# Joined turns between stages, and the tokens' places made on TensorE at the attention's end

## Chip, core and metric

One core of a Trainium2 chip runs the whole program as one launch. The metric is the device time of one execution in microseconds (us). Three executions of the kernel before took 1667.34 (the median), 1662.26 and 1670.05 us.

## What is computed

The input x has 2048 tokens of 512 float32 numbers. Two layers follow each other:

```python
xn = layernorm(x)
x = x + attention(xn) + ffn0(xn)     # layer 0
xn = layernorm(x)
x = x + lightning(xn) + ffn1(xn)     # layer 1

# attention: 16 heads of 32, causal softmax with ALiBi, then @ Wo + bo
# ffn0: each token goes to one of two experts, by a sign:
top_expert = argmax(softmax(xn @ Wg.T))
out0 = gelu(xn @ W0a.T + b0a) @ W0b.T + b0b
out1 = relu(xn @ W1a.T + b1a) @ W1b.T + b1b
y = where(top_expert == 0, out0, out1)
# lightning: chunked linear attention with decay, gate, norm, @ Wo
# ffn1: w1, w2, w3 are rounded to -1, 0, 1 (x1, x2 -> sigmoid(x1) * x2 -> w3)
```

The experts are not both computed for each token. The tokens are sorted by expert into 17 tiles of 128 places (each expert's tokens fill whole tiles, empty places are left at the ends), and `rt.idx`, 128 x 17 whole numbers, says for each place which token lies there, or a dump row past the tokens where none does.

## The kernel before

Six stages run one after the other. Each is a `Stage`, which holds its tiles and semaphores, with one block, in which every engine (PE, DVE, ACT, POOL, SP) has its own program:

- qkv (0 to 168 us): layer norm of x and the three projections. For each of four chunks of 512 tokens it stores xn, q, k (in two parts, high and low) and v to HBM, and loads the first pair of heads' q and k back. At its end SP waits until all stores have landed.
- att (168 to 792 us): the attention, 8 pairs of heads, 40 steps a pair, 320 steps `g` in all. First, `unit` products on PE with their row maxima on DVE (L1030) run ahead by 28 steps (`LEAD`); DVE turns the maxima of a chunk, and SP moves them by small DMAs (L844) into the rows of q, so that the `score` products (L952) come out with the maximum taken off. DVE masks the diagonal (L1039), ACT takes the exponent (L1008), and PE multiplies by v (L966, `sums`). Units and scores share a ring of 7 PSUM banks in an order written out by `ScoreRing`: PE, DVE and ACT all follow it, each product waits until its two banks are free. Pair 0 makes its own units and those of pair 1 within its 40 steps. After the last step's units, some 28 steps before the end, DVE has only masks to do. ACT copies a chunk's sums out (L992), SP stores them. POOL meanwhile loads the second pair's q and k, splits 16 pieces of expert weights into high and low parts (L151, L160) and rounds w1, w2, w3 (`Quantizer`, L202 to L265).
- proj (793 to 870 us): the output projection with the residual, stored as x1a. POOL fetches the first two tiles of xn by `rt.idx`.
- moe (871 to 1098 us): the experts, tile by tile. POOL gathers rows of xn and of x1a and puts the results back by `rt.idx` with indirect DMAs.
- lin (1099 to 1426 us): the linear attention. glu (1427 to 1672 us): ffn1.

A stage ends so: `nc.Block()` closes with a barrier of all engines, ahead of which each engine, POOL too, runs a DRAIN (L55); then POOL clears the stage's semaphores (L57), and a second barrier of all engines follows (L58).

The routing (`Router`) lies in the attention. SP loads its constants (L731, L732) at the start. DVE counts the tokens of expert 0 (L737 to L743) before it takes its first unit, PE makes the ranks with three products (L752 to L754) after the first 12 units, DVE takes them (L760), and after unit 40 DVE makes each token's place in 12 small steps (L768 to L779). POOL fills `token_of_place` in HBM with dump rows (L785), scatters the token numbers to it, 16 indirect DMAs of 128 numbers of 4 bytes (L789), waits for them and loads the table back into `rt.idx` (L792). Only then does it start on the weights. DVE uses `rt.idx` first in proj (L1272).

Of the kernel before, what the change touches and what calls it, by code (L numbers as in the profile page):

```python
# [18 lines left out]
BF16 = mybir.dt.bfloat16  # L19
# [5 lines left out]
P = 128  # L25
T = 2048
# [18 lines left out]
class Stage:  # L45


    def __init__(self, nc, name):
        self.nc, self.name, self.stack, self.sems = nc, name, ExitStack(), []
# [20 lines left out]
    def block(self):  # L70
        return self.stack.enter_context(self.nc.Block())
# [285 lines left out]
class Early:  # L357
# [7 lines left out]

    @staticmethod
    def operands(t):
        return t[0:KROWS, 1, :].rearrange("p (h t) -> p h t", h=2)
# [25 lines left out]
def normed_qkv_stage(nc, early, carried, w_d, bqk_d, bv_d, x_d, cst_d, wg_d, diff, xn_d, qh_d, ql_d, kh_d, kl_d, v_d, alibi):  # L394
# [3 lines left out]
    with Stage(nc, "qkv") as st:  # L398
        wh, wl = st.sb("wh", [P, KT, 2 * D], F32R), st.sb("wl", [P, KT, 2 * D], F32R)
# [13 lines left out]
        vb = st.sb("vb", [P, TT, D])  # L413
# [11 lines left out]
        v_stored = st.sem("v_stored")  # L425
# [5 lines left out]
        def _(sp):  # L431
# [33 lines left out]
            for sem, n in [(xn_stored[i], NCH // 2) for i in range(2)] + [  # L465
                    (qk_stored[i], NCH * 2 * NQK // 4) for i in range(4)] + [
                    (v_stored, NCH), (pair_in, NCH * 2 * LOADS)]:
# [146 lines left out]
LEAD, FIRST_LEAD, PLACES_AT = 28, 12, 40  # L614
# [49 lines left out]
class ScoreRing:  # L664
# [42 lines left out]
class Router:  # L707


    PAD, PARTS = 16, 5  # L710

    def __init__(self, st, rt, room, cst_d, ids_d, dump_d, idx_d, out):
        self.rt, self.cst_d, self.ids_d, self.dump_d, self.idx_d, self.out = rt, cst_d, ids_d, dump_d, idx_d, out
        cst, work = room
        self.cst = cst[:, 0:2 * P + NT + QT]
        self.tri, self.ones = cst[:, 0:P], cst[:, P:2 * P]
        self.starts, self.token = cst[:, 2 * P:2 * P + NT], cst[:, 2 * P + NT:2 * P + NT + QT]
        n = self.PARTS * (self.PAD + QT)
        self.counts_all = work[:, 0:n]
        self.counts = work[:, 0:n].rearrange("p (a b) -> p a b", a=self.PARTS)  # L720
        self.rank, self.place = work[:, n:n + NT], work[:, n + NT:n + NT + QT]
        self.base = work[:, n + 2 * NT:n + 2 * NT + 1]
        self.ids, self.pos = st.sb("ids", [P, QT], U32), st.sb("pos", [P, QT], U32)
        self.cst_in, self.ids_in = st.sem("route_cst_in"), st.sem("route_ids_in")
# [3 lines left out]
        self.filled, self.scattered, self.idx_in = st.sem("route_filled"), st.sem("route_scattered"), st.sem("route_idx_in")  # L728

    def load(self, eng):  # L730
        eng.dma_start(self.cst, self.cst_d).then_inc(self.cst_in, 16)  # L731
        eng.dma_start(self.ids[:], self.ids_d).then_inc(self.ids_in, 16)  # L732
# [14 lines left out]
    def ranks(self, pe):  # L747
# [4 lines left out]
        pe.matmul(self.out[:, 0:QT], self.tri, self.counts[:, 0, pad:], start=True, stop=False)  # L752
        pe.matmul(self.out[:, 0:QT], self.ones, self.counts[:, 4, pad - 1:pad - 1 + QT], start=False, stop=True)
        pe.matmul(self.out[:, QT:NT], self.ones, self.counts[:, 4, pad + QT - 1:pad + QT], start=True, stop=True  # L754
                  ).then_inc(self.ranked, 1)

    def take_ranks(self, dve):

        dve.wait_ge(self.ranked, 1)
        dve.tensor_copy(self.rank, self.out[:, 0:NT]).then_inc(self.rank_taken, 1)  # L760

    def places(self, dve):

        rt, first = self.rt, self.counts[:, 0, self.PAD:]
        dve.wait_ge(self.rank_taken, 1)
        rank = self.rank[:, 0:QT]
        chain = Chain(dve, self.step, 0)
        chain.link(dve.tensor_scalar(rt.f0[:], self.starts, self.rank[:, QT:NT], None, ALU.is_lt))  # L768
# [10 lines left out]
        dve.tensor_copy(self.pos[:], self.place).then_inc(self.placed, 1)  # L779

    def store(self, pool):

        by_place = self.idx_d.rearrange("(j p) a -> p (j a)", p=P)
# [1616 lines left out]
```

## Time and profile before

| | us |
|---|---|
| median of three executions | 1667.34 |
| profiled execution | 1674.07 |
| its span, first to last instruction | 1672.3 |
| mean granted clock of PE | 0.969 of full |
| PE busy | 1547.4 (93%) |
| DVE busy | 985.3 (59%) |
| POOL busy | 658.8 (39%) |
| ACT busy | 591.8 (35%) |

Busy time is the time in which the engine had an instruction under way; PE's ends are modelled. The granted clock has two levels here: 1.00 is 2.4 GHz, 0.50 is 1.2 GHz. In a timeline a row is one instruction, or several alike in a row (x8), with start and duration; the bracket tells how long the engine stood idle before it, and what ended that. SPq, ACTq and POOLq rows are work of the engines' queues (DMA issues, semaphores, DRAINs).

### The profile page before, as it was taken

The page shows a single profiled execution, that of the slowest core. Times are in us where ns is not written, and L with a number is a line of the kernel's source. Part 1 is how long each engine was busy: PE and PEld are TensorE (multiplying, and loading weights), DVE is VectorE, ACT ScalarE, POOL GpSimd, SP SyncE. Part 2 cuts the span into 40 slices and gives each one's busy share as a digit, 9 for nine tenths or more (in the row PEclk, how much of TensorE's full clock was granted, in tenths as well). Part 3 has the DMA queues.
Part 4 walks back from the last instruction along what each step waited for, and adds up shares of the span by engine and source line. Part 5 has one row for each costly group of instructions (what it writes and reads, how often), then busy time and mean ns, then how long its engine had stood idle before and what let it go on. Part 6 is the DMA issues. An engine that isn't in the chain of part 4 may idle for free. (4 is left out here: it accounts for less than half of the span.)

```text
span 1672.3 us, 22094 instructions
## 1 busy us (share of the span) xinstructions
PE 1547.4 (93%) x7890; PEld 1077.2 (64%) x7890; DVE 985.3 (59%) x1706; ACT 591.8 (35%) x1124; POOL 658.8 (39%) x552
## 2 busy tenths in 40 slices
PE   5998969999999999998889999949999998999998
PEld 4887534555555555543667888837777776788887
DVE  7673867878878887770436656535655546232332
ACT  3121224555555555546212222244424232222221
POOL 4100237695885979670318676613110201000000
PEclk9999689999999999999899999979999999999999
DMA  6877513645545464320762122153030222420210
GB/s 235 248 253 210 104 39 97 155 97 121 148 105 102 117 166 101 82 90 11 254 217 69 64 80 66 51 176 122 8 127 0 77 58 81 145 79 22 101 51 25
DMA packets 105053, 182.03 MB, mean 109 GB/s; under 512 B 29433, under 2 KB 45833, under 8 KB 104293
## 3 DMA queue, kind: packets, MB, share of 16 engines
q1 hardware_dynamic: 87176, 119.13, 25.1%
q0 software_dynamic: 14128, 53.88, 11.2%
q10 hardware_dynamic: 3640, 7.61, 1.2%
q8 instruction: 65, 1.06, 0.3%
q14 instruction: 44, 0.35, 0.1%
HBM read 118.56 MB, written 61.75 MB: 108 GB/s over the span
## 5 line engine op out<-in xcount | busy, mean ns | idle before, releaser
L1008 ACT ACTIVATE att_probs<-att_ring 128x512 f32<-128x512 f32 (+3 forms) x640 | 297.0, 538 | 297.9 <-DVE att_ring L1039 172.2
L1030 DVE TENSOR_REDUCE att_maxes<-att_ring 128x2 f32<-128x1024 f32 (+7 forms) x366 | 338.9, 946 | 71.4 <-PE att_ring L931 62.9
L966 PE MATMUL att_outp<-att_probs,att_vs 128*64 128x512 f32 (+3 forms) x1280 | 274.7, 551 | 0.3 <-ACT att_att L992 0.3
L966 PEld LDWEIGHTS att_outp<-att_probs,att_vs 128*64 128x64 f32 x1280 | 78.9, 138 | 122.0 <-issue 69.1
L931 PE MATMUL att_ring<-route_wbh,route_wah 100*128 100x512 f32 (+2 forms) x320 | 103.8, 408 | 12.3 <-PEq L58 6.4
L1731 DVE TENSOR_TENSOR glu_hid<-glu_sig,glu_u 128x512 f32<-128x512 f32 x44 | 30.2, 687 | 141.3 <-PE glu_u L1671 141.3
L931 PE MATMUL att_ring<-moew_wbl,moew_wal 100*128 100x512 f32 (+2 forms) x320 | 98.0, 381 | 15.4 <-ACT att_probs L1008 12.1
L952 PE MATMUL att_ring<-route_wah,route_wbh 102*128 102x512 f32 (+2 forms) x320 | 105.8, 406 | 3.5 <-issue 2.4
L952 PE MATMUL att_ring<-moew_wal,moew_wbl 102*128 102x512 f32 (+2 forms) x320 | 100.9, 399 | 2.6 <-DVE att_maxes L1030 2.5
L2301 POOL TENSOR_TENSOR lin_sig<-lin_o_copy,lin_sig 128x512 f32<-128x512 f32 x16 | 20.4, 1276 | 208.5 <-ACT lin_o_copy L2161 208.5
L1039 DVE TENSOR_TENSOR att_ring<-att_ring,route_cst 128x128 f32<-128x128 f32 x256 | 64.5, 297 | 59.2 <-PE att_ring L952 51.8
L952 PEld LDWEIGHTS att_ring<-route_wah,route_wbh 102*128 102x128 f32 x320 | 55.4, 193 | 67.1 <-issue 44.9
L952 PEld LDWEIGHTS att_ring<-moew_wal,moew_wbl 102*128 102x128 f32 x320 | 53.7, 188 | 63.6 <-issue 32.1
L1744 POOL DMA_DIRECT2D out<-glu_y x3 | 2.4, 798 | 218.0 <-DVE glu_y L1715 218.0
L931 PEld LDWEIGHTS att_ring<-route_wbh,route_wah 100*128 100x128 f32 x320 | 63.5, 206 | 31.8 <-DVE att_maxes L1030 8.7
L931 PEld LDWEIGHTS att_ring<-moew_wbl,moew_wal 100*128 100x128 f32 x320 | 60.1, 191 | 32.2 <-ACT att_probs L1008 17.5
L1542 POOL TENSOR_SCALAR moe_r<-moe_z,route_f 128x512 f32<-128x512 f32 x34 | 69.8, 2057 | 4.1 <-DVE moe_z L1468 2.7
L1670 PE MATMUL glu_u<-tail_xh,tail_up 128*128 128x512 f32 x176 | 68.5, 389 | 2.0 <-DVEq L1723 2.0
L1683 PE MATMUL glu_down<-glu_w,glu_hh 128*128 128x512 f32 x176 | 68.6, 390 | 0.4 <-DVE glu_hl L1733 0.4
L1684 PE MATMUL glu_down<-glu_w,glu_hl 128*128 128x512 f32 x176 | 68.5, 389 | 0.0
L1671 PE MATMUL glu_u<-tail_xl,tail_up 128*128 128x512 f32 x176 | 68.5, 389 | 0.0
L1670 PE MATMUL glu_u<-glu_xh,tail_up 128*128 128x512 f32 x176 | 68.5, 389 | 0.0
(282 smaller groups left out, 3443.4 us busy)
## 6 DMA issues: line engine op xcount, KB each, us to landing
att_q_raw<-in_w POOLq DMA_DIRECT2D x48, 352.0 KB, 3.9
w_ternary<-att_q_out POOLq DMA_DIRECT2D x24, 352.0 KB, 2.6
tail_up<-w_ternary SPq DMA_DIRECT2D x22, 256.0 KB, 4.8
xn<-qkv_x SPq DMA_DIRECT2D x4, 1024.0 KB, 7.3
q_hi<-qkv_hi SPq DMA_DIRECT2D x16, 256.0 KB, 3.8
q_lo<-qkv_lo SPq DMA_DIRECT2D x16, 256.0 KB, 4.7
k_hi<-qkv_hi SPq DMA_DIRECT2D x16, 256.0 KB, 2.9
k_lo<-qkv_lo SPq DMA_DIRECT2D x16, 256.0 KB, 3.7
```

The source lines that it names most:

```text
L931: last = pe.matmul(out[h][:, 0:cover], qs[par][0:SROWS, h, t * P:(t + 1) * P], ks[par][0:SROWS, h, g * CH:g * CH + cover], start=True, sto ...
L952: last = pe.matmul(out[h][:, start:CH], ks[par][:, h, kt * P:(kt + 1) * P], qs[par][:, h, c * CH + start:(c + 1) * CH], start=True, stop=True)
L966: last = pe.matmul(outp[v_cols(h), off:CH], vs[p % 2][:, kt, v_cols(h)], probs[:, g % 4, h, off:CH], start=kt == 0, stop=kt == TT * (c + 1 ...
L1008: act.activation(probs[:, g % 4, h, off:CH], ring[:, rg.banks["score", g][h], off:CH], ACT.Exp).then_inc(exped, 1)
L1030: last = dve.tensor_reduce(maxes[:, hs, t, g:g + 1], banks[:, :, 0:width], AX.X, ALU.max)
L1039: dve.tensor_tensor(block, block, neg_k, ALU.add).then_inc(masked, 1)
L1542: pool.tensor_scalar(r[:, half, :], z[:, half, :], 0.0, rt.f1[:, j:j + 1], ALU.max, ALU.mult).then_inc(relued, 1)
L1670: pe.matmul(u[:, n % 2, :], w[:, f, k, :], xh[c % 2][:, k, :], start=k == 0, stop=False)
L1671: last = pe.matmul(u[:, n % 2, :], w[:, f, k, :], xl[c % 2][:, k, :], start=False, stop=k == KT - 1)
L1683: pe.matmul(down[:, t, :], hh[:, n % 2, s], w3[:, f, :], start=f == 0, stop=False)
L1684: last = pe.matmul(down[:, t, :], hl[:, n % 2, s], w3[:, f, :], start=False, stop=f == GT - 1)
L1731: dve.tensor_tensor(hid[:, n % 2, :], sig[:, n % 2, :], u2[:, n % 2, :], ALU.mult).then_inc(hid_ready, 1)
```

## The change

1. The turns: `Block(no_gpsimd_drain=True)` closes a block with a barrier ahead of which POOL runs no DRAIN. The stage's semaphores are no longer cleared behind that barrier: they are collected, and POOL clears them at the start of the next block, while the other engines already run. The second barrier is gone (one is left at the program's end).
2. Two stores are waited for later. v of the last chunk: not at qkv's end, but in att, by SP ahead of its first load of v, and by POOL ahead of the weights. x1a of the last half chunks: not at proj's end, but in moe, by ACT, DVE and POOL ahead of what reuses the tile or reads x1a.
3. The routing moves from the attention's start into its last 16 steps. The count comes after the mask of step 303, the ranks' products ahead of score 304, and at once DVE makes the places, now 20 steps and a take. Ahead of score 315 PE makes the table itself: for each of 16 tiles of tokens one product of a 128 x 128 matrix of zeros and ones (which lane a token's place has) by 51 columns, in bfloat16, summed over the tiles. DVE takes the sums and joins them to `rt.idx` in four steps. The constants are loaded at step 282 into v's tile of the pair that is done. The table in HBM, its filling, 16 scatters and its load are gone, and so is POOL's wait for them.

```diff
     def __exit__(self, *a):
         self.stack.__exit__(*a)
-        if self.sems:
-            self.nc.clear_and_free_semaphores(self.sems)
-            self.nc.all_engine_barrier()
+        Stage.spent += self.sems
     def block(self):
-        return self.stack.enter_context(self.nc.Block())
+        Stage.clear(self.nc)
+        return self.stack.enter_context(self.nc.Block(no_gpsimd_drain=True))
...
-LEAD, FIRST_LEAD, PLACES_AT = 28, 12, 40
+RANKS_AT, PLACES_AT = NPAIR * NS - QT, NPAIR * NS - TT - 1
+LEAD, FIRST_LEAD = 28, 12
...
         for g in range(NPAIR * NS):
+            if g == RANKS_AT:
+                self.order.append(("ranks", 0))
+            if g == PLACES_AT:
+                self.order.append(("places", 0))
             self.order.append(("score", g))
...
-        dve.tensor_copy(self.pos[:], self.place).then_inc(self.placed, 1)
+        chain.link(dve.tensor_tensor(self.passed, by_tile(self.place, NT + 1), over_tiles(self.starts, NT + 1), ALU.is_ge))
+        chain.link(dve.tensor_reduce(rank, self.passed[:, :, 0:NT], AX.X, ALU.add))
+        chain.link(dve.tensor_tensor(self.passed[:, :, 0:NT], self.passed[:, :, 0:NT], self.passed[:, :, 1:NT + 1],
+                                     ALU.subtract))
+        chain.link(dve.tensor_scalar(rank, rank, -float(P), float(P), ALU.mult, ALU.add))
+        chain.link(dve.tensor_tensor(rank, rank, self.place, ALU.add))
+        whole = self.passed[:, :, 0:NT]
+        dve.tensor_tensor(tiles, whole, by_tile(self.tile, NT), ALU.mult).then_inc(self.placed, 1)
+        dve.tensor_scalar(lanes, whole, self.token[:, 0:1], None, ALU.mult).then_inc(self.placed, 1)
+        dve.tensor_copy(ones, whole).then_inc(self.placed, 1)
+        dve.tensor_tensor(self.lanes, by_tile(rank, P), over_tiles(self.lane, P), ALU.is_equal).then_inc(self.placed, 1)
-    def store(self, pool):
...
-            pool.indirect_dma_start(self.idx_d, bass.IndirectOffsetOnAxis(ap=self.pos[:, t:t + 1], axis=0),
-                                    self.ids[:, t:t + 1], None).then_inc(self.scattered, 16)
...
+    def sum_places(self, pe):
+        pe.wait_ge(self.placed, 4)
+        for t in range(QT):
+            last = pe.matmul(self.out[1][:, 0:self.COLS], self.lanes[:, t, :], self.cols[:, t, :], start=t == 0, stop=t == QT - 1)
+        last.then_inc(self.summed, 1)
...
+            sp.wait_ge(early.v_stored, NCH * 16)
             load_values(sp, 0, v_in[0])
-            router.load(sp)
...
+                if p == NPAIR - 1 and g % NS == COPY_AT:
+                    sp.wait_ge(summed, p * NS)
+                    router.load(sp)
...
-            router.count(dve)
...
+                if (kind, n) == ("score", RANKS_AT - 1):
+                    dve.wait_ge(summed, (NPAIR - 1) * NS)
+                    dve.wait_ge(ws.lo_done, len(ahead))
+                    router.count(dve)
+                if kind == "ranks":
+                    router.take_ranks(dve)
+                    router.places(dve)
+                if kind == "places":
+                    router.take_sums(dve)
+                    router.join(dve)
...
-            router.store(pool)
+            pool.wait_ge(early.v_stored, NCH * 16)
...
+            act.wait_ge(w.x1a_stored[1], QT // 4 * 16)
...
+            dve.wait_ge(w.x1a_stored[0], QT // 4 * 16)
...
+            for i in range(2):
+                pool.wait_ge(w.x1a_stored[i], QT // 4 * 16)
             fetch_rows(0)
```

## Rows read from the trace of the kernel before

**Rows 1.** Windows: length, busy PE PEld DVE ACT POOL, PE clock, DMA share, GB/s.

```profile
185.00:195.00 10.00, 10.00 (x31) 5.70 (x31) 8.22 (x15) 2.01 (x6) 4.90 (x9) 0.52 0.36 81
240.00:260.00 20.00, 9.96 (x35) 4.20 (x34) 7.52 (x17) 3.66 (x9) 8.11 (x8) 0.74 0.13 11
```

**Rows 2.** Instructions of L55 and L58 from 786 to 794 us: ns min/median/max, first and last start.

```profile
L55 ACTq COMPARE_BRANCH  x1: 42/42/42, 792.0 to 792.0; - x1
L55 ACTq EVENT_SEMAPHORE  x1: 17/17/17, 792.4 to 792.4; - x1
L58 ACTq EVENT_SEMAPHORE  x1: 17/17/17, 793.1 to 793.1; - x1
```

**Rows 3.** Instructions of L55 and L58 from 1090 to 1100 us.

```profile
L55 POOLq DRAIN  x1: 4046/4046/4046, 1094.1 to 1094.1; - x1
L58 ACTq EVENT_SEMAPHORE  x1: 17/17/17, 1098.9 to 1098.9; - x1
```

**Rows 4.** Timeline at the turn qkv to att (start, duration, engine, line, operation, idle before).

```profile
163.13 0.38 SPq L464 DMA_DIRECT2D v<-qkv_vb  x1
168.79 0.77 PE L931 MATMUL att_ring<-route_wbh,route_wah 100*128 100x256 f32 x2 [6.42 <-PEq L58]
```

**Rows 5.** Timeline at the turn proj to moe.

```profile
867.60 0.36 SPq L1200 DMA_DIRECT2D x1a<-proj_y  x1
871.44 0.35 SPq L1331 DMA_DIRECT2D moe_ba<-in_ba  x1
876.33 1.23 DVE L1493 TENSOR_TENSOR moe_ba<-moe_ba 128x1024 f32<-128x1024 f32 x1 [2.40 <-DMA moe_ba<-in_ba]
```

**Rows 6.** Timeline at the turn lin to glu.

```profile
1427.54 0.47 PE L1670 MATMUL glu_u<-tail_xh,tail_up 128*128 128x512 f32 x1 [1.97 <-DVEq L1723]
```

**Rows 7.** Timeline of DVE at the attention's start.

```profile
170.75 1.89 DVE L1030 TENSOR_REDUCE att_maxes<-att_ring 128x2 f32<-128x256 f32 x3
196.06 2.09 DVE L1030 TENSOR_REDUCE att_maxes<-att_ring 128x2 f32<-128x768 f32 x2 [2.68 <-PE att_ring L936]
```

**Rows 8.** Timeline of DVE: first step of the places, first unit after them.

```profile
225.10 0.20 DVE L768 TENSOR_SCALAR route_f<-att_q_raw 128x17 f32<-128x17 f32 x1
227.55 0.43 DVE L1026 TENSOR_TENSOR att_ring<-att_ring,route_cst 128x256 f32<-128x256 f32 x1
```

**Rows 9.** Timeline, 228 to 252 us: the first scatter, and DVE's two long waits.

```profile
228.50 1.06 POOL L789 DMA_INDIRECT token_of_place<-att_ids,att_pos  x1 [30.22 <-DVE att_pos L779]
242.90 0.43 DVE L1026 TENSOR_TENSOR att_ring<-att_ring,route_cst 128x256 f32<-128x256 f32 x1 [3.71 <-issue]
251.35 0.50 DVE L1039 TENSOR_TENSOR att_ring<-att_ring,route_cst 128x128 f32<-128x128 f32 x2 [7.29 <-remote]
```

**Rows 10.** Timeline of ACT: copies of sums at steps 14 and 26, 94 and 106.

```profile
222.74 0.60 ACT L992 ACTIVATE att_att<-att_outp 128x512 f32<-128x512 f32 x1 [2.06 <-PE att_outp L966]
262.71 0.60 ACT L992 ACTIVATE att_att<-att_outp 128x512 f32<-128x512 f32 x1 [0.33 <-PE att_outp L966]
...
386.22 0.62 ACT L992 ACTIVATE att_att<-att_outp 128x512 f32<-128x512 f32 x1
407.79 0.60 ACT L992 ACTIVATE att_att<-att_outp 128x512 f32<-128x512 f32 x1 [0.33 <-PE att_outp L966]
```

**Rows 11.** Timeline of the attention's end: steps 302, 304 and 314; and PE's small products.

```profile
764.06 0.89 DVE L1039 TENSOR_TENSOR att_ring<-att_ring,route_cst 128x128 f32<-128x128 f32 x4 [1.84 <-PE att_ring L952]
765.96 1.20 PE L952 MATMUL att_ring<-moew_wal,moew_wbl 102*128 102x512 f32 x4
780.11 1.20 PE L952 MATMUL att_ring<-moew_wal,moew_wbl 102*128 102x512 f32 x4
...
181.54 0.56 PE L754 MATMUL att_outp<-att_q_raw 128*128 128x1 f32 x2
221.60 0.29 PE L936 MATMUL att_ring<-route_neg_q,route_ident 128*128 128x128 bf16 x2
```

**Rows 12.** One line's instructions: ns min/median/max.

```profile
L1052 DVE CAST att_turned<-att_negmax x32: 174/177/2395, 174.3 to 750.8; 128x8 fp32r<-128x8 f32 x32
```

More of the change, by code:

```diff
@@ L45 @@
 class Stage:
+    spent = []
     def __init__(self, nc, name):
@@ L707, with __init__, take @@
 class Router:
[L710 to L717, printed above, removed]
-        n = self.PARTS * (self.PAD + QT)
[L719 to L724, printed above, removed]
+    PAD, PARTS, COLS = 16, 5, 3 * NT
+    def __init__(self, st, rt, room, lanes, cst_d, out):
+        self.rt, self.cst_d, self.out = rt, cst_d, out
+        taken = [0]
+        def take(n):
+            taken[0] += n
+            return room[:, taken[0] - n:taken[0]]
+        self.cst = take(2 * P + NT + 1 + 2 * QT + P + NT)
+        cuts = np.cumsum([0, P, P, NT + 1, QT, QT, P, NT])
+        self.tri, self.ones, self.starts, self.token, self.tile, self.lane, self.dump = (
+            self.cst[:, int(i):int(j)] for i, j in zip(cuts[:-1], cuts[1:]))
+        n = self.PARTS * (self.PAD + QT)
+        self.counts_all = take(n)
+        self.counts = self.counts_all.rearrange("p (a b) -> p a b", a=self.PARTS)
+        self.rank, self.place, self.base = take(NT), take(QT), take(1)
+        self.passed = take(QT * (NT + 1)).rearrange("p (t j) -> p t j", t=QT)
+        self.lanes = lanes[:, 0:QT * P // 2].bitcast(BF16).rearrange("p (t r) -> p t r", t=QT)
+        self.cols = take(QT * (self.COLS + 1) // 2).bitcast(BF16).rearrange("p (t n) -> p t n", t=QT)[:, :, 0:self.COLS]
+        self.sums, self.empty = take(self.COLS), take(NT)
+        self.cst_in = st.sem("route_cst_in")
         self.cleared, self.counted = st.sem("route_cleared"), st.sem("route_counted")
@@ new lines, in take_sums, with join @@
+    def take_sums(self, dve):
+        dve.wait_ge(self.summed, 1)
+        dve.tensor_copy(self.sums, self.out[1][:, 0:self.COLS]).then_inc(self.sums_taken, 1)
+    def join(self, dve):
+        tiles, lanes, ones = (self.sums[:, i * NT:(i + 1) * NT] for i in range(3))
+        dve.wait_ge(self.sums_taken, 1)
+        chain = Chain(dve, self.joined, 0)
+        chain.link(dve.tensor_tensor(self.empty, ones, self.dump, ALU.mult))
+        chain.link(dve.tensor_tensor(self.empty, self.dump, self.empty, ALU.subtract))
+        chain.link(dve.scalar_tensor_tensor(out=tiles, in0=tiles, scalar=float(P), in1=lanes, op0=ALU.mult, op1=ALU.add))
+        chain.link(dve.tensor_tensor(self.rt.idx[:], tiles, self.empty, ALU.add))
@@ L914, in wait_freed @@
                     pe.wait_ge(exped, rg.score_done(*before[1:]))
+                if before and before[0] == "ranks":
+                    pe.wait_ge(router.rank_taken, 1)
+                if before and before[0] == "places":
+                    pe.wait_ge(router.sums_taken, 1)
             def unit_product(v):
@@ L1165, in projection_stage @@
         hi_ready, lo_ready = st.sem("hi_ready"), st.sem("lo_ready")
-        made, added, stored = st.sem("made"), st.sem("added"), [st.sem(f"stored{i}") for i in range(2)]
+        made, added, stored = st.sem("made"), st.sem("added"), w.x1a_stored
         clamped, gathered = st.sem("clamped"), st.sem("gathered")
```

77 lines of the change are left out of this document (40 added, 37 removed).

## The prediction, made before the changed kernel ran

> **What bounds the kernel now.** I read the windows of PE first. PE is the engine that is nearly always busy, but its clock is not always full: in the attention's first stretch it is granted 0.52, that is 1.2 GHz, and it is busy for all 10.00 us of it; from 240 to 260 us it is busy for half of the time, at 0.74 [rows 1]. Outside such places this change touches nothing that PE does, so its worth is read place by place: at the five turns, where all engines stand; at the attention's start and its steps 14 to 26, where the old routing lies; and at the attention's end, where the new one goes. For a turn the instructions of L55 to L58 are the view, for the rest the timeline. Read the turn into proj: ACT leaves its last wait (for a store) at 792.0, the block's barrier lets it go at 792.4, the second barrier at 793.1 [rows 2]. So a turn costs 0.4 us for the first barrier and 0.7 for the clearing and the second, after whatever the last engine waited for.
>
> **The turns.** Each loses the 0.7 us between the barriers; the clearing itself goes to POOL's start, where POOL waits for loads or other engines anyway.
> - qkv to att. SP issues the last store of v at 163.13 (to 163.51) and PE starts again at 168.79 [rows 4]; the store's landing lies between. Without that wait, SP is the last at the barrier, and with 0.4 for it and 0.1 for the last semaphores PE starts at 164.05: 4.7 us gained. SP now waits for v in att, to about 167.7 (168.79 less the two barriers). Behind it in SP's queue stand the load of v and the row moves of chunk 0; these are wanted when DVE has its first maxima, which is later, so nothing waits. POOL comes to its wait for v at about 198 (228.50 less its wait of 30.22 [rows 9]), long after it landed.
> - att to proj: 0.7. lin to glu: 0.75, from the row in which PE had stood 1.97 us [rows 6].
> - proj to moe. The store of x1a is issued at 867.60 (to 867.96), the first load of moe at 871.44 [rows 5]. With 0.4 and 0.1 that load goes out at 868.4: 3.0 us. All of moe's start follows its own loads (DVE stands until ba lands, 876.33), so it moves as a whole. The added waits for x1a stand behind instructions that run after 876; the store landed at about 870.4 (871.44 less 0.3 and the 0.7). Free.
> - moe to lin. POOL's DRAIN takes 4046 ns after the last store has landed, from 1094.1, and the others are let go at 1098.9 [rows 3]. Without it: 4.05 and 0.7, 4.75 us. lin's start is loads and DVE work that follow the turn. If the clearing at lin's start holds the same DRAIN, it delays POOL alone, whose first work in lin waits for weights that ACT rounds behind its loads.
>
> Sum of the turns: 4.7 + 0.7 + 3.0 + 4.75 + 0.75 = 13.9 us. The end keeps both barriers.
>
> **The attention's start.** DVE counts before it takes the first unit: it starts on units at 170.75 [rows 7], PE has the first at 169.56 [rows 4]. The count gone: 1.1 us (at least 0, at most 1.9, its length). Then the clock. PE had stood 6.42 us and works at 1.2 GHz until 195 [rows 1, 4]; after a stand of 1.97 us it did its next product in 0.47 us, which is full speed [rows 6]. With a stand of 1.6 us I expect the full clock here. What that is worth is not half of 26 us, since DVE is busy for 8.22 of 10 us beside it [rows 1]; what goes is DVE's waiting, above all the 2.68 us before 196.06 [rows 7]. I take 2.7; bounds 0 (clock stays down) and 4.5 (that and the rest of DVE's 1.78 us). Ranks taken off PE there: nothing, DVE is behind. Sum 3.8 us.
>
> **Steps 14 to 26.** The places take DVE from 225.10 to 227.55 [rows 8], with PE waiting for units and then at the lower clock for some products: 2.45 for the steps, 1.3 for the clock, 3.7 in all (bounds 2.4 and 5). Then the stand-still: while POOL issues its 16 scatters, from 228.50 on, DVE waits 3.71 us and then 7.29 us, for nothing that the trace names, and PE, ACT and DVE all stand [rows 9]. Nothing of this sort is in the other pairs: the 12 steps from 94 to 106 take 21.6 us, those from 14 to 26 40.0 us [rows 10]. Two more units (2.1 us, from the 768 wide maxima, 2.09 for two [rows 7]) and the places explain 5.8 of the difference of 18.4; 12.6 are left. I put down 11 to the scatters: both waits less the 1 us each that such waits usually are, and 2 for the lower clock behind them. Bounds 0 and 12.6. The sum here: 14.7 us.
>
> Two sentences of the Trainium skill speak against this. "SBUF — State Buffer", section "SBUF: two separate sides", says that engine ports and DMA ports are separate and that a compute operation can't be slowed by a DMA; by that the scatters are innocent and the stand-still would come again, which is the first rival below. The trace agrees in no other place or against it; it only shows that both come together once.
>
> **POOL's work moves.** It starts on the weights at least 30 us earlier, the wait ahead of its first scatter [rows 9]. It ends before the attention does in both kernels, so this frees nothing. The same work meets the same kind of DVE work, earlier.
>
> **The attention's end.** Here DVE is idle but for masks, and PE and ACT follow each other closely, so what PE waits or does more goes to the end nearly whole.
> - Ranks. The masks of steps 302 and 303 end at 764.95, and PE goes on to score 304 at 765.96 [rows 11]. The count then begins at 764.95: six small steps, each 0.2 from start to start as the first of the places [rows 8], 1.3 us with the clearing, then PE's three products. Six halves of them took 1.25 us at 1.2 GHz (the last row, 0.56 for two), so 0.65 at full clock. Score 304 comes at 767.0 to 767.5: 1.3 us later (bounds 1.0 and 2.5).
> - Places. From there DVE has one take, 11 old steps (2.4 us), five wide ones of some 280 numbers (0.4 each, 2.0), three small ones (0.6) and the comparison of 2048 numbers (2.8, by the 768 wide maxima at 1.04 [rows 7]): 8.0 us, done at about 775.5. PE came to scores 314 and 315 at 780.11 [rows 11], and comes 1.3 later. DVE is in time, with 6 us to spare.
> - The table on PE: 16 products with 128 bfloat16 rows; two such with 128 columns took 0.29 us [rows 11], so 16 take 1.6 to 2.3 us. ACT has the exponents of step 314 beside it. I take 1.5 us (bounds 0.5 and 3).
> - Joining takes 1 us of DVE, ahead of the mask of step 316, which comes 3 us later. The constants' load at step 282 is behind nothing.
>
> Sum: 2.8 us lost (bounds 1.5 and 5.5).
>
> **The sum.** 13.9 + 3.8 + 14.7 - 2.8 = 29.6 us gained. From the profiled execution's own 1674.07 that is 1644.5. That execution lies 6.7 us above the median of the runs shown, and the three runs 7.8 apart. If the excess were in what stays, the median would come to 1637.7; if it is the stand-still, it is gone already. I take 1642.
>
> **The rivals.**
> 1. The stand-still is not the scatters' (for it: the rule above, and that no instruction of POOL or DMA is named as the releaser; against: it is there once in 320 steps, and there the scatters are). Then 18.6 us are gained: 1655.5 from the profile, 1648.7 from the median, I say 1652.
> 2. The end costs more: the places aren't done when PE comes to score 315. DVE's steps would have to take 14 us in place of 8; every microsecond beyond is a whole one, and PE could fall to 1.2 GHz behind such a stand. At 2.5 times my length, 20 us, PE waits 6 and does its last five steps at the lower clock, 4 more: 1652. Against it: DVE's small steps are 0.2 us from start to start [rows 8], and POOL has no work left there.
> 3. Slower. POOL's 16 pieces now lie over steps of pair 0 where DVE has two units a step. One small DVE step between tiles in SBUF takes 177 ns as a rule and once 2395 [rows 12]. By the same page and section of the Trainium skill, a DVE operation and a POOL operation that want the shared pair of ports exclude each other for a whole instruction; that agrees with this one row. As a mechanism of this kernel: some 50 masks and small steps of DVE lie there, I estimate; if each waited 0.5 us more, the 25 us between the forecast and the median before would be spent, and at 0.7 us the time is 1677. Against it: the same line took its median in nearly all of its 32 runs, most of them beside POOL, and at the other end POOL leaves as much earlier.
> 4. The change doesn't do all that it says: the block's end still waits for POOL's DRAIN, or PE's clock stays at 1.2 GHz in the attention's start. 4.05 and 2.7 us less: 1645 to 1649, within the forecast's range.
>
> **How the numbers follow.** The forecast, with rival 4 in it, has 0.65, and its own range is 1636 to 1650; rival 1 has 0.22, rival 2 0.10, rival 3 0.03. The range takes in rival 1 from either base nearly whole, and the better base at the low end: 1632 to 1654. What can be told from no change is 0.5%, 8.3 us: faster is below 1659.0, slower above 1675.7. All of the forecast is faster, of rival 1 nine tenths, of rival 2 most: 0.92. Same 0.06, slower 0.02.
>
> **What would show it.** In the new trace: first products of att about 1.6 us behind qkv's last, at clock 1.00 in the first 25 us; no POOL DRAIN of 4 us at a turn, and 4 us from moe's last DMA issue to lin's start where there were 8; first moe load within 1 us of the last store's issue; steps 14 to 26 in 24 to 26 us, with no wait of DVE over 2 us; score 304 behind DVE's count by 0.7 us, and PE's 16 products ahead of score 315 without a wait for DVE. I am wrong if a wait of 7 us stands in pair 0 again, if score 304 to score 314 takes over 17 us (14.15 now [rows 11]), or if a POOL instruction stands in the chain at lin's start.

## The result, and the profile after

The kernel after took 1654.3 us in the median of nine executions (1649.5 to 1658.3), the kernel before 1667.3 in nine beside them (1657.5 to 1674.0): ratio 0.9928, 95% interval 0.9903 to 0.9952, 12 to 13 us less. The gain is more than the 0.5% from which a change can be told, but half of the 25 us that were forecast, and the time lies just above the range of 1632 to 1654. The profiled execution after took 1654.82 us, 19.3 less than the profiled one before. The gap between 19.3 and 13 is where the search began.

The turns did what was said. Timeline of the kernel after, turn qkv to att: the last store of v, then PE 1.93 us behind qkv's last product, where it had stood 6.42 [rows 4]. PE was released at 164.27, the forecast said 164.05.

```profile
163.09 0.39 SPq L475 DMA_DIRECT2D v<-qkv_vb  x1
164.27 0.48 PE L992 MATMUL att_ring<-route_wbh,route_wah 100*128 100x256 f32 x2 [1.93 <-PEq L58]
```

Turn proj to moe, same view. The first load goes out 1.13 us behind the store's issue (3.84 before [rows 5]).

```profile
852.68 0.36 SPq L1271 DMA_DIRECT2D x1a<-proj_y  x1
853.81 0.35 SPq L1400 DMA_DIRECT2D moe_ba<-in_ba  x1
858.94 1.23 DVE L1563 TENSOR_TENSOR moe_ba<-moe_ba 128x1024 f32<-128x1024 f32 x1 [3.10 <-DMA moe_ba<-in_ba]
```

Turn moe to lin. Between POOL's last DMA and SP's first load lie 3.2 us. No DRAIN of 4 us stands there any more [rows 3].

```profile
1075.62 1.00 POOL L1622 DMA_INDIRECT x<-moe_y,route_idx  x1 [6.67 <-DVE moe_y L1559]
1078.82 1.75 SPq L1948 DMA_DIRECT2D tail_y<-x  x4
1091.67 1.94 PE L2008 MATMUL lin_ring<-lin_cst,tail_y 128*128 128x128 f32 x8 [17.05 <-DMA lin_g<-in_Wg]
```

Windows (length, busy PE PEld DVE ACT POOL, PE clock, DMA share, GB/s). The first answers to [rows 1] at the attention's start: the clock is 0.66 in its first ten microseconds and 0.90 later, not 1.00 as forecast, but not 0.52 either. The third is the stretch of the old stand-still, 0.74 before.

```profile
170.00:180.00 10.00, 8.64 (x28) 5.86 (x28) 9.86 (x17) 1.09 (x2) 0.00 (x0) 0.66 0.12 25
185.00:195.00 10.00, 9.58 (x43) 4.99 (x41) 7.95 (x10) 4.31 (x9) 6.75 (x13) 0.90 0.99 200
240.00:260.00 20.00, 19.43 (x87) 10.04 (x87) 13.70 (x20) 12.02 (x25) 12.39 (x16) 1.00 0.54 118
```

The attention's end, DVE and PE in the timeline: the count, three products of the ranks, score 304 at 751.02 (0.8 behind the last counting step, which ends at 750.21; 0.7 was said), the large comparison done at 758.88, and the 16 products in 0.60 us ahead of the second half of a score, without a wait.

```profile
748.97 0.19 DVE L764 MEMSET att_vs<- 128x160 f32 x1
749.40 0.81 DVE L770 TENSOR_TENSOR att_vs<-att_vs 128x16 f32<-128x16 f32 x4
756.59 2.29 DVE L824 TENSOR_TENSOR att_wstage<-att_vs 128x2048 bf16<-128x2048 f32 x1
750.80 0.36 PE L781 MATMUL att_ring<-att_vs 128*128 128x1 f32 x2
751.02 1.17 PE L1013 MATMUL att_ring<-moew_wal,moew_wbl 102*128 102x512 f32 x4
765.72 0.60 PE L830 MATMUL att_ring<-att_vs,att_wstage 128*128 128x51 bf16 x16
```

### The profile page after: what moved, and what is told of

Read it like the earlier page. It is cut to its first block and busy times, and to the rows that moved or that the text cites. A ratio compares the mean times of both kernels' runs of the same rounds, so it can differ in the third digit from the quotient of the medians.

```text
span 1653.0 us, 22088 instructions
## 1 busy us (share of the span) xinstructions
PE 1547.6 (94%) x7906; PEld 1077.0 (65%) x7906; DVE 997.4 (60%) x1719; ACT 593.1 (36%) x1124; POOL 640.0 (39%) x534
## 5 line engine op out<-in xcount | busy, mean ns | idle before, releaser
L992 PEld LDWEIGHTS att_ring<-route_wbh,route_wah 100*128 100x128 f32 x320 | 61.6, 199 | 27.7 <-DVE att_maxes L1094 10.7
L211 POOL TENSOR_SCALAR att_q_above<-att_q_raw 128x704 f32<-128x704 f32 x24 | 61.6, 2568 | 19.4 <-DMA att_q_raw<-in_w 18.7
```

Of the source, the lines that this page charges most:

```text
L211: step(pool.tensor_scalar(self.above[:], x, 0.0, 2.0, ALU.max, ALU.mult))
L992: last = pe.matmul(out[h][:, 0:cover], qs[par][0:SROWS, h, t * P:(t + 1) * P], ks[par][0:SROWS, h, g * CH:g * CH + cover], start=True, sto ...
```

## The experiments

Eighteen runs were made, some of them of the same kernel. A time is the median of the kernel's executions, "before" is the kernel before beside it on the same chip; a ratio has its 95% interval. Each group of runs below was made on one chip, in one session; no chip was used twice. Steps are counted by ACT's copies of the sums, as in [rows 10].

### One part alone, and the scatters alone

Turns alone: the kernel before with parts 1 and 2 of the change, of which the core is this; routing alone: the kernel after with the same taken back.

```diff
-            self.nc.clear_and_free_semaphores(self.sems)
-            self.nc.all_engine_barrier()
+        Stage.spent += self.sems
...
-        return self.stack.enter_context(self.nc.Block())
+        Stage.clear(self.nc)
+        return self.stack.enter_context(self.nc.Block(no_gpsimd_drain=True))
...
+            sp.wait_ge(early.v_stored, NCH * 16)
```

Without scatters:

```diff
-        for t in range(QT):
-            pool.indirect_dma_start(self.idx_d, bass.IndirectOffsetOnAxis(ap=self.pos[:, t:t + 1], axis=0),
-                                    self.ids[:, t:t + 1], None).then_inc(self.scattered, 16)
-        pool.wait_ge(self.scattered, QT * 16)
...
-    dump = T + np.arange(NT * P)[:, None]
+    dump = np.arange(NT * P)[:, None]
```

> The kernel before with parts 1 and 2 of the change alone (joined clearing, one barrier a turn, no DRAIN of POOL, both stores waited for later); the routing stays as it was, with its 16 scatters. Theory A, the prediction's: 13.9 us for the turns and 2.7 for the clock at the attention's start, 16.6 us faster than before in the median. Theory B, the routing's move brings nothing in the median, since the stand-still of the profiled execution is not the scatters': the turns alone bring all that was measured, 13 us. Theory C, moe and lin give back what their start gains (seen in the two traces, 2.1 and 1.6 us): 16.6 less 3.7, 13 us as well, but then the routing's move must be worth less than nothing or nothing.

> The kernel before with part 3 of the change alone (count, ranks and places in the attention's last 16 steps, the table on PE, no scatters); the turns stay as they were, with both barriers, the DRAIN and the waits for both stores. Theory A: the scatters cost 11 us in the median too, so this is 1.1 + 14.7 less 2.8, 13 us faster. Theory B: the stand-still is not the scatters', so what is left is 1.1 and 3.7 less 2.8, 2 us faster. Theory C, the end costs more than 2.8: within 1 us of before, or slower.

> The kernel before without the 16 indirect DMAs that scatter the token numbers, and without the wait for them: the table is filled by its constant alone, which here holds the numbers 0 to 2175, so each token lies at its own place and some tokens meet the wrong expert. All the rest, the places on DVE too, is as before. Theory A (the scatters make the stand-still): 11 us faster in the median, and no wait of DVE over 2 us in steps 14 to 26. Theory B (they do not): within 2 us of before in the median, and waits of several us still appear somewhere in the attention in its profile.

> The kernel before, unchanged: a second profile of it, and what a comparison of a kernel with itself gives here. Theory A: the two waits of 3.7 and 7.3 us stand behind the scatters again. Theory B: waits of some us stand in other steps of the attention, or none at all does, and steps 14 to 26 take about 29 us (21.6, and 5.8 for the two more units, the places and the clock, and the rest by chance).

Before took 1680.5 us on this chip, 13 more than on the first. Turns alone: 1669.1, ratio 0.9947 (0.9919 to 0.9976). Routing alone: 1668.2, 0.9918 (0.9891 to 0.9945). Without scatters: 1666.1, 0.9917 (0.9888 to 0.9946). Before again: 1682.0, 1.0006 (0.9980 to 1.0032). So here the scatters cost 14 us, theory A, and the two parts together should have brought 23 us by the ratios (9 and 14 us; 11 and 12 by the medians), not 13. The profiles said the same: steps 14 to 26 took 40.0 us in before again and 40.6 with the turns alone, 26.9 and 28.2 in the two without scatters. What stands there is not an instruction of DVE or ACT that got longer. DVE in the profile of turns alone (timeline), all inside POOL's 16 scatters:

```profile
239.06 1.23 DVE L1038 TENSOR_REDUCE att_maxes<-att_ring 128x2 f32<-128x1024 f32 x1 [5.98 <-remote]
244.00 0.43 DVE L1034 TENSOR_TENSOR att_ring<-att_ring,route_cst 128x256 f32<-128x256 f32 x1 [3.71 <-remote]
247.61 0.50 DVE L1047 TENSOR_TENSOR att_ring<-att_ring,route_cst 128x128 f32<-128x128 f32 x2 [2.45 <-remote]
```

Three waits, 12.1 us together, where rows 9 have two of 11.0, and in other places of the step order; the reductions last 1.23 us as ever. Rival 1's mechanism and theory B fell with the kernel without scatters, which is 14 us faster and has no such wait.

Whose releases come late stands in the semaphore events of the traces. In the profile of the kernel before, PE has four score products on record as ended at 240.58, 240.82, 241.88 and 244.55; the updates of their semaphore, counted in order, come at 251.33, 251.36, 251.44 and 251.47. In the three other profiles with a stand-still in which all 640 updates of that semaphore are on record, the longest lag of one is 9.4 to 10.7 us; in the eleven without a stand-still it is 0.02 us. DVE's release is not late in the same stretch: the last of those products starts at 244.11, 0.05 us behind the end of the DVE reduction that it waits for. So what is held is PE's work or the news of it, and DVE and ACT stand for want of that. Since PE's ends are modelled, the traces don't tell which of the two it is, and what holds it is not shown.

### Both parts on another chip, and what POOL's rounding costs

In the second and third kernel the rounding of w1, w2, w3 is loads and stores only. Each piece is loaded once there and not twice, so some DMA work goes with the arithmetic:

```diff
-                if k == 0:
-                    magnitude(self.below[:], self.raw[0][:])
...
+                pool.dma_start(pieces_of(q_d)[k], self.raw[k % 2][:]).then_inc(self.stored, 16)
+                pool.wait_ge(self.stored, (n + 1) * 16)
```

The fourth is the kernel after with one instruction exchanged:

```diff
-                    ins = dve.tensor_copy(split[:, 0].bitcast(F32R), negmax[:])
+                    ins = dve.tensor_reduce(split[:, 0].bitcast(F32R), maxes[:, :, c * TT:(c + 1) * TT, 0:c + 1], AX.X, ALU.max,
+                                            negate=True)
```

> The kernel after, unchanged, on the chip and in the rounds of the three below: turns alone brought 0.53% (9 us) and the routing's move alone 0.82% (14 us) against before. Theory A, both parts add up: 22 us faster, ratio 0.987. Theory D, together they are worth less than their sum, since something that one part brings is lost when the other is there: 13 us faster as first measured, ratio 0.992. In its profile, theory E (POOL, which starts on the weights 30 us earlier without the scatters, meets DVE's two small steps between tiles in SBUF at each turn of the maxima) expects steps 26 to 266 over 440 us again, where the kernels with the scatters had 436, 439 and 441.

> The kernel after without POOL's arithmetic in the rounding of w1, w2, w3: the pieces are only loaded and stored, so the last layer works with unrounded weights. POOL keeps its 16 pieces of expert weights. Theory E: DVE's two small steps of a turn of the maxima keep to 0.2 us after the first 100 us of the attention, each pair takes 71 us, and the attention is 8 to 20 us shorter than in the kernel after. Rival F, the pairs' spread (71 to 77 us) has another cause, such as DMA or the clock: it stays, and the time is within 3 us of after.

> The kernel before with the same arithmetic of POOL left out. Theory E: the collisions cost less here than after, so this gains some 6 us less over before than the kernel above gains over after, and the two differ by 20 us or more: the part of the change's worth that was lost is back. Theory A: both gain the same, and the two differ as before and after do.

> The kernel after with one instruction changed: DVE's copy of the negated maxima into their rounded high part (a CAST from SBUF to SBUF) is made by a second reduction of the maxima instead. By the Trainium skill, page SBUF — State Buffer, section on its two separate sides, a copy can take the port pair that DVE shares with POOL and a reduction cannot. Theory E, from rows: the 32 copies took 26 us in the kernel after in place of 6, so up to 16 of them waited over 0.3 us; without them the attention is 4 to 10 us shorter. The second small step, a subtraction of two tiles in SBUF, still waits. Rival F: no difference, or slower by 1 us, since the reduction takes as long as a copy and the waits lie where DVE has time.

Before took 1666.8 here. After again: 1654.0, ratio 0.9936 (0.9913 to 0.9959), theory D as it seemed. Without the rounding's arithmetic: after 1641.3, before 1654.1, that is 12.7 and 12.6 less than with it, and the same 12.8 between them. So POOL's rounding, its second loads included, costs 12 to 13 us in both kernels alike. The part of theory E that was to explain the missing gain (the collisions cost more after the change) is wrong. That most of the cost is collisions, the next kernel speaks for; it was not run without the rounding as well.

The reduction: 1644.0, ratio to before 0.9880 (0.9853 to 0.9907), 10 us faster than after. Its rows, grouped by line and form, beside those of the kernel after. After:

```profile
L1116 DVE CAST att_turned<-att_negmax 128x8 fp32r<-128x8 f32 x32 | 25.8, 806 | 1.1
L1118 DVE TENSOR_TENSOR att_turned<-att_negmax,att_turned 128x8 fp32r<-128x8 f32 x32 | 10.7, 333 | 0.3
```

Another profile of that kernel, on the chip of the one with the reduction:

```profile
L1116 DVE CAST att_turned<-att_negmax 128x8 fp32r<-128x8 f32 x32 | 18.2, 568 | 1.1
L1118 DVE TENSOR_TENSOR att_turned<-att_negmax,att_turned 128x8 fp32r<-128x8 f32 x32 | 16.8, 526 | 0.1
```

With the reduction, its widest and its narrowest form:

```profile
L1116 DVE TENSOR_REDUCE att_turned<-att_maxes 128x8 fp32r<-128x32 f32 x8 | 1.5, 189 | 0.3
L1116 DVE TENSOR_REDUCE att_turned<-att_maxes 128x8 fp32r<-128x8 f32 x8 | 1.4, 170 | 0.3
L1119 DVE TENSOR_TENSOR att_turned<-att_negmax,att_turned 128x8 fp32r<-128x8 f32 x32 | 14.2, 444 | 0.1
```

The copy took 806 and 568 ns in the mean of the two profiles, the reduction of up to four times as many numbers 170 to 189. The copy is in the chain from the maxima to the scores of the next chunk, so DVE's wait becomes PE's.

### The two parts, taken apart where executions lie close together

All four without the rounding's arithmetic, on one chip (before, with it, took 1664.8). The turns alone got one wait more, of POOL for its own last weight piece.

> The kernel before without POOL's arithmetic in the rounding of the weights, once more: the base for the three below, in which the same is left out, since the executions of such kernels lie closer together (after: 3 us). Theory G (the stand-still behind the scatters comes in some executions only): its single times spread over 8 us or more, and its profile has either steps 14 to 26 in 40 us, or, as the last such profile, in 27.5. Theory A: always 40 us.

> Turns and deferred stores alone, against the one above. Theory A, the prediction's: 16.6 us faster (13.9 and 2.7 for the clock). Theory H: each turn gives what was said (4.6, 0.4, 2.9, 4.8, 0.7 in the profiles, 13.4), but PE's clock gives part of it back: it comes back to full no earlier after a stage's end, so that moe and lin start on it at 1.2 GHz for longer, 1.5 us each, and POOL's gathers in moe 1 us; 10 us faster.

> The routing's move alone, against the first. Theory A: 13 us faster (1.1 and 14.7 less 2.8). Theory G, where most executions have no stand-still: 3 us (steps 6 to 26 3 us shorter, the start 1.5, the end 1.6 longer), and its times spread over 3 us where the kernel with the scatters has 8.

> Both, against the first. If the two parts do not disturb each other, it is faster by the sum of the two above. From the last rounds I expect 13 us: 10 of the turns and 3 of the routing (theories H and G); theory A expects 29.

| | routing as before | routing moved |
|---|---|---|
| turns as before | 1654.5 (1651.5 to 1656.9) | 1651.4 (1650.4 to 1652.4) |
| turns joined | 1639.6 (1636.2 to 1641.7) | 1641.4 (1639.4 to 1642.5) |

The turns bring 14.9 us with the old routing and 10.0 with the moved one, the routing's move 3.1 us with the old turns and -1.8 with the joined ones. So on this chip the change is its turns, and they and the routing share some 5 us that either brings and both bring once. Half of that is to be seen in the profiles: steps 26 to 42 take 33.0 us with neither part (33.5 and 33.4 in the two other profiles of that kernel), 30.8 with the turns alone, 30.8 with the routing alone, 30.5 with both. (In an execution of the kernel before with its rounding and no stand-still, they take 30.9, as little as with the parts, so for the kernel that was forecast this share is not shown.) In both profiles here that have the 16 scatters, steps 14 to 26 take 27.5 and 27.6 us, with no stand-still (theory G).

### Is it the chip?

Three profiles with scatters had shown the stand-still and three not. The first three had the rounding and ran where before takes 1680 us or was profiled at 1674; the others had no rounding and ran elsewhere. The next six runs separate the two.

> The kernel before, unchanged, a third profile. Theory G1 (the stand-still goes with the chip or the execution): on a chip where before takes 1665 us, steps 14 to 26 take 27.5 us with all 16 scatters in them, as in the three kernels without the rounding's arithmetic. Theory G2 (the stand-still needs the rounding, and those three kernels had none for that reason): 40 us again.

> The kernel before without the 16 scatters and the wait for them (each token at its own place), on another chip than the first time, when it was 14.5 us faster than before. Theory G1: if before has steps 14 to 26 in 27.5 us here, the scatters cost nothing, and it is within 3 us of before. Theory G2 and A: 10 to 14 us faster again.

> The kernel after with the reduction in place of DVE's copy, once more, beside the next: 10 us faster than after the first time, 22 us faster than before. I expect 20 to 23 us faster than before again.

> Turns and deferred stores with the same reduction, but the routing as before, scatters and all. Where before shows no stand-still (theory G1) the routing's move is worth -2 to 3 us, and this one is within 3 us of the one above. Where it shows it, this one is 10 to 14 us slower than the one above.

Before took 1679.9 on this chip. Its third profile: steps 14 to 26 in 39.9 us. Without scatters: 1669.3, ratio 0.9935 (0.9907 to 0.9962). After with the reduction: 1643.4, 0.9790 (0.9759 to 0.9820), 36 us less than before, where it was 23 less on the earlier chip, at the same time of its own (1644.0). Turns with the reduction and the old routing: 1656.1, 0.9858 (0.9836 to 0.9881), 12.8 slower than the one beside it, by the scatters and their stand-still (39.9 us in its profile too).

> The kernel before, unchanged, a fourth profile, beside the next on one chip. So far the kernels with scatters took 13 us longer on two chips (before 1680 us) than on three others (1665 to 1667), those without them took the same on all (1643 to 1644 for the one with the reduction). Theory G1 (the chip decides): where before takes 1665 us, steps 14 to 26 take 27.5 us; where it takes 1680, 40 us. Theory G2 (the rounding's arithmetic decides): 40 us on any chip.

> The kernel before without the arithmetic of the rounding, on the same chip. Theory G1: steps 14 to 26 take what they take in the kernel above, 27.5 us on a chip of 1665 us and 40 us on one of 1680, where this kernel then takes 1667 us. Theory G2: 27.5 us on any chip, beside 40 us above, and 1655 us or less.

Before took 1663.2 here, and before once more 1665.0 (ratio 1.0009, 0.9983 to 1.0035); without the rounding's arithmetic 1652.9 (0.9922, 0.9895 to 0.9948). Steps 14 to 26: 27.5 us in the kernel before, rounding and all, and 27.6 in the other. That rules out theory G2 and is what G1 says. ACT's copies of steps 14 and 26, the kernel before on the chip of 1680 us:

```profile
223.83 0.60 ACT L992 ACTIVATE att_att<-att_outp 128x512 f32<-128x512 f32 x1 [2.05 <-PE att_outp L966]
263.76 0.60 ACT L992 ACTIVATE att_att<-att_outp 128x512 f32<-128x512 f32 x1 [0.32 <-PE att_outp L966]
```

and on the chip of 1663 us:

```profile
220.25 0.60 ACT L992 ACTIVATE att_att<-att_outp 128x512 f32<-128x512 f32 x1 [2.04 <-PE att_outp L966]
247.75 0.60 ACT L992 ACTIVATE att_att<-att_outp 128x512 f32<-128x512 f32 x1 [0.32 <-PE att_outp L966]
```

The same kernel, the same 20 us of its attention. Windows, on the chip of 1680 us:

```profile
236.00:256.00 20.00, 9.97 (x38) 4.34 (x36) 7.04 (x15) 4.65 (x9) 10.71 (x12) 0.77 0.12 18
```

and on the chip of 1663 us:

```profile
236.00:256.00 20.00, 19.97 (x91) 10.09 (x88) 15.96 (x32) 10.39 (x24) 7.74 (x9) 1.00 0.47 73
```

PE is busy for half of the first stretch and all of the second. The DMAs move 18 GB/s in place of 73; whether they are held as well, or only not asked for since the engines stand, these rows don't tell. The scatters themselves are issued at the same pace on both, and take 10.6 and 8.6 us in the median from issue to landing. First and last issue, and the load that waits for their landing (timeline of POOL), chip of 1680 us:

```profile
229.59 1.06 POOL L789 DMA_INDIRECT token_of_place<-att_ids,att_pos  x1 [27.95 <-DVE att_pos L779]
...
248.84 0.97 POOL L789 DMA_INDIRECT token_of_place<-att_ids,att_pos  x1 [0.30 <-issue]
255.96 1.35 POOL L792 DMA_DIRECT2D route_idx<-token_of_place  x1 [6.14 <-DMA token_of_place<-att_ids,att_pos]
```

and chip of 1663 us:

```profile
226.02 1.06 POOL L789 DMA_INDIRECT token_of_place<-att_ids,att_pos  x1 [28.01 <-DVE att_pos L779]
...
245.21 0.97 POOL L789 DMA_INDIRECT token_of_place<-att_ids,att_pos  x1 [0.30 <-issue]
260.46 1.35 POOL L792 DMA_DIRECT2D route_idx<-token_of_place  x1 [14.28 <-DMA token_of_place<-att_ids,att_pos]
```

Where all else stands still, POOL's wait for the last landing is 8 us shorter. What differs is open. In all nine profiles of the experiments that have the scatters the stand-still goes with the chip (four with it on two chips, five without it on three), but each chip was used in one session, so it may be something of the session and not of the chip. How many chips are of either kind is open too: two took 1680 us, the three others of the experiments 1663 to 1667. The kernel after, as it stands, was timed beside a before of 1667 us both times and took 1654; on a chip of 1680 us only its form with the reduction ran.

## Why the prediction was wrong, step by step

**The step that failed** is the stand-still: "I put down 11 to the scatters", and from it "if it is the stand-still, it is gone already. I take 1642." The mechanism was right: where the stand-still is, the scatters make it, and without them it is gone. What failed is where the term was put down. It was in the profiled execution, of 1674 us, and by all signs not in the executions that made the median of 1667: where profiles show it the kernel before took 1680 us, where they don't 1663 to 1667, and the gain of 13 us came again on a chip of 1667. (Of those executions themselves there is no profile of the kernel before, so this is inferred.) The term of 11 belongs to a chip of the first kind, where the scatters cost 14 and 11 us in two measurements and the two parts measured alone bring 9 and 14 us, near the 25 forecast. On the others steps 14 to 26 take 27.5 us with the scatters in them, and 24.5 to 28.2 in the ten profiles without scatters, so the term is near 0. The forecast named the clue itself, 6.7 us between the profile and the median, and then split the difference instead of asking whether the timed runs had the stall at all. Without the term, its own sum from the median gives rival 1's 1648.7. Rival 1 had the better number with the wrong mechanism: a forecast of it would have come nearer by luck.

What is left, 6 us, are the small terms. The figures below are means over the profiles that have a part and those that have not (nine with joined turns, eleven without). Several are smaller than the spread between profiles of one kernel, and are bookkeeping more than proof.

- **The turns**, 13.9 forecast. qkv to att 4.5 (4.7 said), att to proj 0.45 (0.7), proj to moe 2.9 (3.0), moe to lin 4.5 (4.75), lin to glu 0.7 (0.75): 13.0. Each term stands.
- **"All of moe's start follows its own loads, so it moves as a whole"** failed by 2.8 us: moe takes 222.4 us with joined turns (220.8 to 223.3) and 219.6 without (218.5 to 221.9). Of the 2.8 us, 2.4 are there by the second tile's end and all by the third's. One of POOL's first two gathers takes 1.65 to 2.0 us in all nine profiles with joined turns, and 1.5 to 1.9 in three of eleven without; the usual time is 0.95. Before:

```profile
881.54 0.96 POOL L1145 DMA_INDIRECT rows_xg<-xn,route_take  x1
882.80 0.95 POOL L1145 DMA_INDIRECT moe_y<-x1a,route_take  x1 [0.30 <-issue]
883.05 1.28 DVE L1459 SCALAR_TENSOR_TENSOR moe_bsel<-moe_ba,route_f 128x1024 f32<-128x1024 f32 x1
886.31 1.12 DVE L1473 SCALAR_TENSOR_TENSOR moe_g<-moe_g,route_f,moe_r 128x512 f32<-128x512 f32 x1 [1.98 <-POOL moe_r L1542]
887.48 0.66 PE L1379 MATMUL moe_ht<-route_cst,moe_g 128*128 128x128 f32 x4 [1.18 <-DVE moe_g L1473]
```

After:

```profile
864.99 1.28 DVE L1529 SCALAR_TENSOR_TENSOR moe_bsel<-moe_ba,route_f 128x1024 f32<-128x1024 f32 x1
865.41 1.67 POOL L1216 DMA_INDIRECT moe_y<-x1a,route_take  x1 [0.30 <-issue]
869.26 1.12 DVE L1543 SCALAR_TENSOR_TENSOR moe_g<-moe_g,route_f,moe_r 128x512 f32<-128x512 f32 x1 [3.00 <-POOL moe_r L1613]
870.44 0.66 PE L1448 MATMUL moe_ht<-route_cst,moe_g 128*128 128x128 f32 x4 [2.20 <-DVE moe_g L1543]
```

  Before, POOL's gather began 0.25 us ahead of DVE's step; after, 0.42 behind it, and lasted 0.7 longer. DVE then waits 3.00 in place of 1.98 for POOL, PE stands 2.20 in place of 1.18. PE works in moe for 10 us or more at 1.2 GHz in six of the nine, and in two of the eleven. That the two collide there was read from the rows and not tried, but the rows of all profiles agree: in the thirteen gathers that began while this DVE step (moe_bsel<-moe_ba,route_f, which reads two tiles in SBUF) was under way, the gather ended 0.82 to 0.85 us after the step's end; where the step began later, the gather took 0.95 us.
- **lin** starts at the lower clock for 9 us behind its first product in eight of the nine profiles with joined turns (3.6 before). The window of its start, before and after:

```profile
1112.00:1122.00 10.00, 7.25 (x32) 5.88 (x33) 2.67 (x4) 6.86 (x14) 3.94 (x4) 0.79 0.29 105
```

```profile
1091.00:1101.00 10.00, 7.36 (x24) 5.77 (x25) 2.77 (x4) 6.59 (x12) 3.56 (x3) 0.50 0.26 93
```

  In this pair of profiles lin's products, first to last, take 2.2 us longer. Over all profiles it is 0.2, since six of the eleven without the joining started as slowly.
- **The attention's start**, 3.8 forecast, is 1.2: the clock comes back in part (0.66 and 0.90 above) and gives 0.5, the count 0.7. "With a stand of 1.6 us I expect the full clock here" failed. The stand was 1.93 us, and PE was at 1.2 GHz for 17 of its first 36 us (26 of them before). Nor is this a gain of the shorter stand for sure: in five other profiles, of kernels with the old turn, the stand was 6.4 us and PE was at 1.2 GHz for 17 to 19 of those 36 us just the same.
- **The places**, 3.7 forecast, are 0.5. Steps 6 to 26 take 50.5 or 50.6 us in all five profiles of kernels with scatters but no stand-still, and 50.1 in the mean of the six with both parts (48.0 to 52.2). So most of DVE's 2.45 us had cost the attention nothing.
- **The end**, 2.8 forecast, is 1.55 us (38.5 for the last two chunks, 36.95 before). The ranks cost what was said; the 16 products took 0.60 us where 1.5 was taken. The lower bound of 0.5 was nearer.
- **POOL's earlier work**: rival 3 is wrong in its sign, but its price was real. POOL's rounding costs 12 to 13 us, before and after alike, and with DVE's copies turned into reductions 10 us went. They were in the base. The forecast's argument against it, that the copy "took its median in nearly all of its 32 runs", misread [rows 12], which have only least, median and most: in that trace 11 of the 32 copies took over 0.3 us, and the mean is 424 ns.

The sum of the measured terms is 13.0, less 2.8 and 0.2 for moe and lin, 1.2 and 0.5 more, less 1.55: 10.2 us. With the 2.6 us of steps 26 to 42, which no step of the forecast had, that is 12.8, and 12 to 13 were timed. The 2.6 us are from the kernels without the rounding alone, and where they come from wasn't tried. With the rounding in the kernel steps 26 to 282 vary by some 10 us between executions, which would hide them, so that the sum meets the timed gain is no proof of it.

The forecast set two sentences of the Trainium skill against itself. "SBUF — State Buffer", section "SBUF: two separate sides", says that engine ports and DMA ports are separate, so that a compute operation can't be slowed by a DMA. Whether the stand-still contradicts it, the traces don't tell: DVE's and ACT's instructions kept their lengths, but PE's products may have been held themselves (by up to 10.7 us, above). The rule is about ports; it does not say that engines can't be held up by DMAs in another way, and I had read it as if it did. The Trainium skill, same page, section "Who interferes with whom", says that a copy can take the port pair that DVE shares with POOL, that a two-tile operation contends with a POOL operation that reads SBUF, and that a reduction on trn2 never contends. The traces agree: copies of 806 and 568 ns in the mean beside POOL's work, reductions of 170 to 189, and the subtraction of two tiles still at 444 where it took 200 without the rounding, on another chip.

## What to carry to other kernels

A profile is one execution on one chip. Where its time stands apart from the median, ask first whether the stall that you price is in the median at all, and forecast from a base of one kind. A view with least, median and most doesn't tell the mean: ask for it. Look at small DVE copies between SBUF tiles on a chain that PE waits for, beside a busy POOL: a reduction in the copy's place brought 10 us here, as much as the whole change's turns, and with it the kernel takes 1643 to 1644 us on both kinds of chip, the fastest version measured that rounds its weights. A joined turn gives what its barriers took, but the stage behind it starts with other neighbours, and may give a fifth of it back.

## What was not expected of the hardware

- While the same 16 indirect DMAs of 128 numbers of 4 bytes are issued, updates of PE's semaphores come up to 10.7 us late, and steps 14 to 26 take some 12 us longer, on two chips (and in the profiled execution before), and nothing of the sort is there on three others.
- The lower clock at a stage's start does not go by the stand ahead of it alone: after a stand of 1.93 us PE still worked at 1.2 GHz for 17 of 36 us, as it did in five profiles for 17 to 19 us after one of 6.4.
- One DVE copy of 8 numbers a row, 0.18 us alone, took 0.57 and 0.81 us in the mean of a whole attention, in two profiles.
- A gather of POOL that starts under a DVE step with two tiles in SBUF ends 0.82 to 0.85 us after that step, 13 times of 13, in place of taking 0.95 us.
